# A four-layer graph network on one core: the node stages keep x in SBUF, project two tiles at a time, collect with five products and load their weights ahead

## The reference

```python
f_s, f_v = lin(s_in, v_in, W1_s, W1_v, attr)      # projection, gathered per edge
sc_s, sc_v = lin(s_in, v_in, W_sc_s, W_sc_v, attr)
w = silu(edge_scalars @ fcW1) @ fcW2
edge_feat = concat([wA*xs*y0, wD*dot(xv, y1), wB*xs*y1, wC*xv*y0])
agg = segment_sum(edge_feat, edge_dst)
conv = lin(agg_s, agg_v, W2_s, W2_v, attr)         # collection
angle = 0.1 * (agg_s @ W3) * attr
x = layernorm(x + cos(angle)*sc + sin(angle)*conv)
```

## Time and profile before

| | us |
|---|---|
| median of 3 runs (lowest, highest) | 10053.95 (10026.35, 10073.98) |
| profiled execution | 10054.84 |
| its span, first to last instruction | 10053.1 |
| TensorE matmul busy | 6317.1 |
| VectorE busy | 5171.9 |
| GpSimd busy | 4066.1 |
| ScalarE busy | 2083.1 |

### The profile page before, as it was taken

One profiled execution on the slowest core, in us unless ns is written; L12 is line 12 of the kernel. 1 busy time (PEld: TensorE's weight loads), 2 busy tenths in 40 slices (PEclk: granted clock), 3 DMA queues, 4 the chain that ended last, 5 costly groups with the idle time before them and its releaser, 6 DMA issues. The chain is left out here.

```text
span 10053.1 us, 161925 instructions
## 1 busy us (share of the span) xinstructions
PE 6317.1 (63%) x45291; PEld 4638.5 (46%) x45292; DVE 5171.9 (51%) x11558; ACT 2083.1 (21%) x5924; POOL 4066.1 (40%) x4048
## 2 busy tenths in 40 slices
PE   3666666656666666666766756756666666566665
PEld 1333333436566656655656645633333353333334
DVE  3455555435555655555555666444444444444444
ACT  2000000124444444444444410100000010000001
POOL 0455555034444444444444400035555523555551
PEclk9777777768778887877778878856666675666667
DMA  4222222122222222222222224312222211222221
GB/s 144 58 60 60 61 60 60 36 60 61 59 64 62 64 63 60 62 60 62 61 63 61 64 73 129 82 53 61 62 61 61 62 41 52 54 53 53 53 54 40
DMA packets 530289, 629.89 MB, mean 63 GB/s; under 512 B 140978, under 2 KB 412530, under 8 KB 530072
## 3 DMA queue, kind: packets, MB, share of 16 engines
q0 software_dynamic: 193920, 331.22, 13.5%
q1 hardware_dynamic: 336280, 297.56, 9.9%
HBM read 526.85 MB, written 101.57 MB: 63 GB/s over the span
## 5 line engine op out<-in xcount | busy, mean ns | idle before, releaser
L829 POOL DMA_INDIRECT e_rows<-tab,e_idx x2424 | 2352.1, 970 | 2404.8 <-DVE e_feat L947 1420.7
L1110 POOL DMA_INDIRECT acc<-tabx,a_idx x1616 | 1666.0, 1031 | 2310.6 <-DVE acc L1292 1119.1
L859 PE MATMUL e_win<-e_feat,e_ohy 128*32 128x96 f32 (+1 forms) x19392 | 1674.3, 365 | 975.5 <-issue 964.5
L859 PEld LDWEIGHTS e_win<-e_feat,e_ohy 128*32 128x32 f32 x19392 | 875.3, 142 | 1744.6 <-issue 1637.6
L874 PE MATMUL e_wps<-e_w,e_hidT 64*128 64x192 f32 (+1 forms) x4848 | 938.1, 511 | 740.2 <-DVE e_hidT L953 594.8
L874 PEld LDWEIGHTS e_wps<-e_w,e_hidT 64*128 64x128 f32 x4848 | 630.3, 282 | 1025.8 <-DVE e_hidT L953 709.4
L844 ACT ACTIVATE e_tanh<-e_hid 128x512 f32<-128x512 f32 x303 | 181.0, 597 | 4279.2 <-DMA x_d<-x_sb 3229.2
L925 DVE SCALAR_TENSOR_TENSOR acc<-e_win,lo,acc 128x160 f32 (+1 forms) x606 | 230.8, 381 | 1593.7 <-DMA acc<-tabx,a_idx 1134.1
L1173 PE MATMUL a_c<-acc,a_buffer 128*128 128x128 f32 (+1 forms) x4848 | 710.9, 293 | 108.2 <-ACT a_buffer L1151 95.6
L1169 PE MATMUL a_tps<-ident_sb,acc 128*128 128x128 f32 (+1 forms) x2424 | 426.0, 304 | 526.7 <-ACT acc L1126 437.2
L1173 PE MATMUL a_scal<-acc 96*128 96x164 f32 x1616 | 504.5, 404 | 365.7 <-ACT acc L1126 270.5
(11 more groups left out here) (244 smaller groups left out, 8322.4 us busy)
## 6 DMA issues: line engine op xcount, KB each, us to landing
h_d<-a_buffer SPq DMA_DIRECT2D x202, 320.0 KB
s_hin<-h_d SPq DMA_DIRECT2D x202, 320.0 KB, 3.3
e_rows<-tab,e_idx POOLq DMA_INDIRECT x2424
e_ein<-in_e64T SPq DMA_DIRECT2D x202, 128.0 KB
acc<-tabx,a_idx POOLq DMA_INDIRECT x1616
a_ein<-e_part SPq DMA_DIRECT2D x404, 48.0 KB
e_ein<-e_part SPq DMA_DIRECT2D x202, 96.0 KB
e_part<-s_parts SPq DMA_DIRECT2D x36, 404.0 KB, 3.1
```

What stands on the lines that cost most here:

```text
L829: pool.indirect_dma_start(out=rows[:, s, t, :], out_offset=None, in_=k.tab0, in_offset=bass.IndirectOffsetOnAxis(ap=idx[:, s, t:t + 1], ax ...
L859: mm = pe.matmul(win[NB * y:NB * (y + 1), s, 0:many * V], ohy[:, s, t, y, :], feat[:, s, t, first:first + (many - 1) * pitch + 1:pitch, :] ...
L1110: pool.indirect_dma_start(out=rows[:, b, q, :], out_offset=None, in_=table, in_offset=bass.IndirectOffsetOnAxis(ap=idx[:, b, end, q:q + 1] ...
```

## The change

x stays in SBUF through the program (`k.x`); `load_x`, the store to `x_d` and the reloads are gone, and x is loaded in `setup`, which also loads layer 0's projection weights and waits for all of it. Later projection weights are loaded in `finish`, the collection's at the end of the edge stage; both stages wait for them. The projection is written out in pairs of tiles: ScalarE does the copies out of PSUM, the 32-row chunk of the second tile goes to partitions 32 to 63 beside a second copy of its weights, the output has three buffers of two PSUM banks, and each store takes a pair. The collection has five products: the 32-feature remainders of the four harmonics are stacked on 128 partitions of `c_st_rest` by four ScalarE copies in layers 0 and 1; in layers 2 and 3 only the last harmonic has such a remainder, one copy fills it and the rest is zero.

```diff
...
-SLOTS = 8
+SLOTS = 5
...
+                sp.dma_start(k.x[:, :, :], a["x"].rearrange("(t p) d -> p t d", p=P)).then_inc(loaded, 16)
+                load_ahead(sp, ahead, loaded)
...
-                v.wait_ge(loaded, 16 * 7)
+                v.wait_ge(loaded, 16 * (8 + len(ahead)))
...
+    pairs = [(t, min(2, n - t)) for t in range(0, n, 2)]
...
-        xT0 = h.sb(name + "xT0", [P, 2, P])
-        xT1 = h.sb(name + "xT1", [V, 2, P])
-        rows = h.sb(name + "rows", [P, 2, TC])
+        w0, w1 = weights.w
+        xT0 = h.sb(name + "xT0", [P, 2, 2, P])
+        xT1 = h.sb(name + "xT1", [2 * V, 2, P])
+        rows = h.sb(name + "rows", [P, 3, 2, TC])
...
+        po = h.ps(name + "po", [P, 3, 2, 512])
...
-                load_weights(sp, loaded, weights, a)
-                sp.dma_start(k.x_d.rearrange("(t p) d -> p t d", p=P), x[:, :, :]).then_inc(x_saved, 16)
...
-                def step(t, s, i):
-                    if not isinstance(t, int) or t >= 2:
-                        hold(act, k, turned, t - 1)
-                    act.activation(xs[:, s:s + 1, :], xin[:, bass.ds(t, 1), :], ACT.Copy).then_inc(staged, 1)
-
-                rounds(act, n, step)
+                for p, (t, many) in enumerate(pairs):
+                    act.wait_ge(turned, p + 1)
+                    act.activation(xT0[:, p % 2, 0:many, :].rearrange("p t n -> p (t n)"), pt[:, p % 2, 0:many * P], ACT.Copy)
+                    for j in range(many):
+                        ins = act.activation(xT1[V * j:V * (j + 1), p % 2, :], pt[0:V, p % 2, (2 + j) * P:(3 + j) * P], ACT.Copy)
+                    ins.then_inc(copied, 1)
...
-                def step(t, s, i):
-                    if inside(t, n):
-                        pe.wait_ge(staged, t + 1)
-                        pe.transpose(pt[:, s, 0:P], xs[:, s, 0:P], k.ident[:, :])
-                        pe.transpose(pt[0:V, s, P:2 * P], xs[:, s, P:D], k.ident[:, :]).then_inc(turned, 1)
-                    if inside(t - 1, n):
-                        if isinstance(t, int) and t == 1:
-                            pe.wait_ge(wready, 1)
-                        pe.wait_ge(copied, t)
-                        pe.matmul(po[:, 1 - s, 0:C], xT0[:, 1 - s, :], w0[:, :], start=True, stop=False)
-                        pe.matmul(po[:, 1 - s, 0:C], xT1[:, 1 - s, :], w1[:, :], start=False, stop=True).then_inc(product, 1)
-
-                rounds(pe, n, step, after=1)
+                def turn(p):
+                    t, many = pairs[p]
+                    if p >= 2:
+                        pe.wait_ge(copied, p - 1)
+                    for j in range(many):
+                        pe.transpose(pt[:, p % 2, j * P:(j + 1) * P], xin[:, t + j, 0:P], k.ident[:, :])
+                    for j in range(many):
+                        mm = pe.transpose(pt[0:V, p % 2, (2 + j) * P:(3 + j) * P], xin[:, t + j, P:D], k.ident[:, :])
+                    mm.then_inc(turned, 1)
+                def products(p):
+                    t, many = pairs[p]
+                    pe.wait_ge(copied, p + 1)
+                    if p >= 3:
+                        pe.wait_ge(drained, p - 2)
+                    for j in range(many):
+                        pe.matmul(po[:, p % 3, j, 0:C], xT0[:, p % 2, j, :], w0[:, :], start=True, stop=False)
+                    for j in range(many):
+                        here = slice(V * j, V * (j + 1))
+                        mm = pe.matmul(po[:, p % 3, j, 0:C], xT1[here, p % 2, :], w1[here, :], start=False, stop=True)
+                    mm.then_inc(product, 1)
+                turn(0)
+                for p in range(len(pairs)):
+                    if p + 1 < len(pairs):
+                        turn(p + 1)
+                    if p == 0:
+                        pe.wait_ge(wready, 1)
+                    products(p)
...
-                scale_weights(v, chain, weights)
+                for w, c in zip(weights.w, weights.c):
+                    chain.link(v.tensor_tensor(w[:, :], w[:, :], c[:, :], ALU.mult))
...
-                        o = 1 - s
-                        hold(v, k, product, t)
-                        if not isinstance(t, int) or t >= 3:
-                            uses = (i - 1 + s) if not isinstance(t, int) else (t - 1) // 2
-                            hold(v, k, stored[o], uses * (16 * len(tables)))
-                        if scaled:
-                            a_t = over(k.attr[:, bass.ds(t - 1, 1)], 2, TC)
-                            v.tensor_tensor(rows[:, o:o + 1, :], po[:, o:o + 1, 0:TC], a_t, ALU.mult).then_inc(rows_ready, 1)
-                            a_t = over(k.attr[:, bass.ds(t - 1, 1)], 2, C - TC)
-                            v.tensor_tensor(k.sc[:, bass.ds(t - 1, 1), 0:C - TC], po[:, o:o + 1, TC:C], a_t, ALU.mult).then_inc(k.held, 1)
-                        else:
-                            v.tensor_copy(rows[:, o, :], po[:, o, 0:TC]).then_inc(rows_ready, 1)
-
...
+                for p, (t, many) in enumerate(pairs):
+                    v.wait_ge(product, p + 1)
+                    if p >= 3:
+                        v.wait_ge(stored[p % 3], 16 * len(tables) * (p // 3))
+                    if L != 1:
+                        a_t = k.attr[:, t:t + many]
+                        v.tensor_tensor(rows[:, p % 3, 0:many, :], po[:, p % 3, 0:many, 0:TC], over(a_t, 2, TC), ALU.mult).then_inc(rows_ready, 1)
+                        v.tensor_tensor(k.sc[:, t:t + many, 0:C - TC], po[:, p % 3, 0:many, TC:C], over(a_t, 2, C - TC),
+                                        ALU.mult).then_inc(drained, 1)
+                    else:
+                        v.tensor_copy(rows[:, p % 3, 0:many, :], po[:, p % 3, 0:many, 0:TC]).then_inc(rows_ready, 1)
+                        v.wait_ge(rows_ready, p + 1)
+                        v.sem_inc(drained)
...
-                    for q, (_, m) in enumerate(chunks):
-                        ins = act.activation(st[0:m, s, q, :, :, :].rearrange("p y b n -> p b y n"),
-                                             tp[0:m, s, q, :].rearrange("p (b y n) -> p b y n", b=4, y=4), ACT.Copy)
+                    act.activation(st[:, s, :, :, :].rearrange("p y b n -> p b y n"),
+                                   tp[:, s, 0, :].rearrange("p (b y n) -> p b y n", b=4, y=4), ACT.Copy)
+                    if every:
+                        for y in range(4):
+                            ins = act.activation(st_rest[NB * y:NB * y + NB, s, :, :],
+                                                 tp[0:NB, s, 1, :].rearrange("p (b y n) -> p y b n", b=4, y=4)[:, y, :, :], ACT.Copy)
+                    else:
+                        ins = act.activation(st_rest[0:rest, s, :, :],
+                                             tp[0:rest, s, 1, :].rearrange("p (b y n) -> p y b n", b=4, y=4)[:, 3, :, :], ACT.Copy)
...
-                        for q, (at, m) in enumerate(chunks):
-                            for b in range(4):
-                                mm = pe.transpose(tp[0:m, s, q, b * P:(b + 1) * P],
-                                                  acc[:, t * 4 + b, at:at + m], k.ident[:, :])
+                        for b in range(4):
+                            pe.transpose(tp[:, s, 0, b * P:(b + 1) * P], acc[:, t * 4 + b, 0:P], k.ident[:, :])
+                        for b in range(4):
+                            mm = pe.transpose(tp[0:rest, s, 1, b * P:(b + 1) * P], acc[:, t * 4 + b, P:P + rest], k.ident[:, :])
...
-                        for q, (_, m) in enumerate(chunks):
-                            for y in range(4):
-                                mm = pe.matmul(po[:, o, 0:C], st[0:m, o, q, y, :, :].rearrange("p b n -> p (b n)"), w[0:m, 4 * q + y, :],
-                                               start=q + y == 0, stop=q == 1 and y == 3)
-                        mm.then_inc(product, 1)
+                        for y in range(4):
+                            pe.matmul(po[:, o, 0:C], st[:, o, y, :, :].rearrange("p b n -> p (b n)"), w[:, y, :], start=y == 0, stop=False)
+                        pe.matmul(po[:, o, 0:C], st_rest[:, o, :, :].rearrange("p b n -> p (b n)"), w[:, 4, :],
+                                  start=False, stop=True).then_inc(product, 1)
...
                     chain.link(v.reciprocal(rden[:, :], rden[:, :]))
-                v.wait_ge(loaded, 16 if heads else 32)
-                scale_weights(v, Chain(v, wlink), weights)
+                else:
+                    chain.link(v.tensor_tensor(w[:, :, :], w[:, :, :], c[:, :, :], ALU.mult))
...
-                sp.dma_start(x[:, :, :], k.x_d.rearrange("(t p) d -> p t d", p=P)).then_inc(loaded, 16)
+                load_ahead(sp, ahead, loaded)
+                sp.wait_ge(loaded, 16 * len(ahead))
...
+                load_ahead(sp, ahead, ahead_in)
+                sp.wait_ge(ahead_in, 16 * len(ahead))
...
-            load_x(nc, k, a, x)
-            project(nc, k, 0, a, x, x, D + 192, [(k.tab0, D)])
...
```

(5 more changed lines are left out.)

164 lines of the change are left out of this document (75 added, 89 removed).

## The result

The changed kernel takes 9732.10 us, the median of four runs (9696.86 to 9754.01), beside 10063.97 for the kernel before on the same chip (four runs, 10026.35 to 10089.79): a ratio of 0.967, 95% interval 0.9626 to 0.9713. The forecast was 9722. The profiled execution took 9737.42, with a span of 9735.6.

What follows compares the result with a forecast made beforehand. No engine fills the whole span; TensorE bounds projections and collections. Projections 182.1, collections 140.2, x's reload 9.7 and setup 0.9 sum to 332.9 us off 10054.8, giving 9722 us, range 9685 to 9840.

Steps and rivals of the forecast that it cites:

- I take the upper level, after two pairs at the lower one: Projections: TensorE reaches 2.4 GHz after two pairs at 1.2 GHz, saving 45.3 us in layer 0, 127.5 in the others.
- the low rival: Projections stay at 1.2 GHz, perhaps because transposes do not count as activity: gain 89.3 for 182.1, so 9815 us; chance 0.18.
- the starts: Projection starts: weights already in SBUF save 3.5 us in layer 0, 2.9 each in layers 2 and 3; 9.3 us.
- the steady pair: Projections at the upper clock: a pair of tiles takes 2.52 us in layer 0 and 2.36 in the others.
- Written-out code: Rival on the projections' instructions: straight-line code fetched too slowly costs 356 us, kernel ends at 10078 us; chance 0.02.
- Row groups overlap: Projections: a pair's four short passes on two row groups cost two; full-price rival 27 us more, short-work chance 0.12.
- Collections: Collection tiles: eight products become five, 2.49 us for 3.82 in layer 0; saves 33.2 us there, 88.5 in the others.
- I take 0.22: Collections of layers 0 and 1: each small ScalarE copy takes 0.22 us, hidden; at 0.57 the kernel takes 9748 us.
- Starts of the collections, 18.5: Collection starts: weights loaded in the messages stage remove waits of 5.5, 5, 5 and 3 us, 18.5 in all.
- x in SBUF: Layer 1's finish loses its 9.7 us wait for x's reload; moving x's load into setup gains 0.9 us.
- at 317 GB/s 2.77 MB are 8.7: Setup: loading x and 0.7 MB of weights adds 8.7 us, replacing the 9.6 us load stage: gain 0.9 us.
- Edge stages, zero: Messages and attention stages: no change was predicted; a messages stage growing over 5 us would count as wrong.

Runs made afterwards that it cites:

- e1: Changed kernel with projection groups of one tile instead of pairs: 7144.79 us, kernel before 7306.74 in that set; projections 85.0, 80.3, 79.7, 79.7 us.
- e3: Changed kernel with a pair's passes ordered long, short, long, short: 7093.80 us, kernel before 7306.74; projections 86.3, 81.6, 46.4, 81.0 us.
- e2: Changed kernel with both short chunks of a pair on one row group: 6992.38 us, one run, kernel before 7306.74; projections 50.5, 42.3, 41.9, 42.2 us.
- e7: Changed kernel with eight products per collection tile again, weights still loaded ahead: 9837.78 us, kernel before 10057.85; collections 365.3 us in sum.
- e8: Changed kernel with ScalarE's small copies in layers 0 and 1's collections made twice: 9755.97 us, one run; those collections 76.5 and 74.8 us.
- e10: Changed kernel with x and layer 0's weights loaded during the scalar-splitting passes, not setup: 6961.24 us, unaltered 6968.62; setup 20.3 us.
- e5: Changed kernel, unaltered, repeated in the second set: 9719.60 us, 338 us under the kernel before, ratio 0.9672.
- e9: Changed kernel, unaltered, repeated in the third set: 6968.62 us, 348 us under the kernel before, ratio 0.9529.
- e11: e10's kernel with projection groups of three tiles, two output buffers, short chunks stacked by products for one copy: 6946.54 us, ratio to kernel before 0.9501.

## Why the prediction was right

**The sum** (9722 against 9732.10, in the range) rests on terms that hold one by one, except as follows. That it came within 10 us is in part luck: the projections gave 12 us more than their term, and the first comparison's scatter took 26 back. In the other sets the gain was 338 and 348 us for the forecast's 332.9.

**Projections, "I take the upper level, after two pairs at the lower one"**: the level was right. e1 shows what the low rival would have cost: 80 us a stage. The two low pairs were too many: in the four stages the first pair took 1.9, 1.2, 0.7 and 1.2 us more than a steady one and the second nothing, 5.0 in sum where the term had 17.6. That is the 12 us by which the term was short; the starts gave 1.6 more than their 9.3, and the steady pair, 2.56 and 2.40 for 2.52 and 2.36, took 0.5 a stage the other way. The number of low pairs varies from run to run (35.3 to 38.4 us for the same code in layers 2 and 3). The argument for the level, a long stretch of full-array work, is what e3 tests: it turns the order, and with it overlap and row changes, and loses three stages of four. The added argument, that the two row groups raise it further, was not needed (e2). Written-out code is no brake: TensorE is busy for 25.00 of 25 us in the first window above. Nor did four transposes in twelve passes keep the clock low, as the rival had it.

**Row groups overlap**, taken from the earlier trace rows: 0.74 us for four passes where e2 has 1.26. Right, 6.5 us a stage.

**Collections**: tile 2.50 for 2.49, and e7 gives 115.6 for the 121.7. "I take 0.22" for a small copy was low, 0.27 apart; it lies under TensorE's work all the same (e8).

**Starts of the collections, 18.5**: too low; beside e7's 115.6 the measured 141.4 leaves 25.8, so one term 6 too high and one 7 too low made the sum nearly exact, which is luck. The clock behind the wait was no term of mine. With five slots the late load is worth only 11.0.

**x in SBUF**: "at 317 GB/s 2.77 MB are 8.7" gave setup +8.7 and it was +9.8, close for half a reason. The loads alone account for 5.6 of it, as the vector part could not have started before they landed; the other 4.2 come from the small stores queued behind them, which the text had named and then costed at nothing. The same bytes cost 1.2 us where e10 puts them.

**Edge stages, zero**: right within their scatter.

## What to carry to other kernels

A gapless TensorE can still run at half clock: compare pass durations with the column count, and try grouping full-array passes of several tiles before the short ones. Take loads out of the start of a stage, since a stall there costs the wait and can cost the clock behind it. Look at what stands behind a large load on the same queue: here a small store left 8.4 us later for it. And put such a load where its landing is not waited for at once; moving it gave 8.0 us.

## What the runs showed of the hardware beyond that

The same program took 7307 and 10058 us in two sets whose records name the same chip. GpSimd's issues in the messages stage, 400 us of e5 and then of e9:

```profile
L840 POOL DMA_INDIRECT e_rows<-tab,e_idx x214 | 212.2, 992 | 189.3 <-DVE e_feat L958 126.8 <-issue 62.4
```
```profile
L840 POOL DMA_INDIRECT e_rows<-tab,e_idx x313 | 305.7, 977 | 95.4 <-issue 95.4
```

An issue takes the same 0.98 to 0.99 us, but in e5 GpSimd waits 126.8 us for buffers that VectorE has yet to read; in e9 it never waits. VectorE and TensorE in the same 400 us of e5:

```profile
L936 DVE SCALAR_TENSOR_TENSOR acc<-e_win,lo,acc 128x160 f32 x53 | 20.3, 383 | 97.4 <-remote 97.4
L870 PE MATMUL e_win<-e_feat,e_ohy 128*32 128x160 f32 x1696 | 144.6, 399 | 69.3 <-issue 68.0
```

In e9 both groups have no idle time before them. A group of 512 edges takes 2.4 us longer in e5 (53 of them in the 400 us against 78), and 1.8 of it is VectorE's wait at L936, which by the code needs TensorE's e_win and no gathered row. At L949, which needs the rows, it waits 92.6 us for 53 groups against 96.0 for 78, 0.5 more a group. So it is not mainly the gathered rows that come late. TensorE's 68.0 us are idle time for which the profile shows no reason; what causes them was not found. The node stages are the same in both.

The granted clock of the first window of the kernel before, 1.00, stands over passes that run at 1.2 GHz. The trace's clock records begin at 254.5 us there and at 157.3 in the changed kernel, and a window ahead of the first record reads 1.00 whatever the passes do. Passes on two or three row groups start together, 7 ns apart in e11: with three, six passes cost the time of two.
